# Turning the exponentials of a softmax through scratch memory and VectorE instead of through TensorE

## What is computed

```python
xn = group_norm(x, gamma, beta)
xf = xn.reshape(B, n, C)                       # n = H * W = 1024
q, k, v = xf @ Wq + bq, xf @ Wk + bk, xf @ Wv + bv
attn = jnp.einsum('bnc,bmc->bnm', q, k) * scale
attn = jax.nn.softmax(attn, axis=-1)
out = jnp.einsum('bnm,bmc->bnc', attn, v)
out = out @ Wp + bp
return xn + out.reshape(B, H, W, C)
```

## Time and profile before

| what | us |
|---|---|
| timed runs, median (lowest to highest) | 1071.11 (1070.84 to 1073.47) |
| profiled execution, its own time | 1070.88 |
| its span | 1068.9 |
| TensorE busy | 1023.6 (96%) |
| VectorE busy | 835.5 (78%) |
| ScalarE busy | 730.4 (68%) |
| GpSimd busy | 395.7 (37%) |

### The profile page before, as it was taken

One profiled execution on the slowest core, in us unless ns is written; L12 is line 12 of the kernel. 1 busy time (PEld: TensorE's weight loads), 2 busy tenths in 40 slices (PEclk: granted clock), 3 DMA queues, 4 the chain that ended last, 5 costly groups with the idle time before them and its releaser, 6 DMA issues.

```text
span 1068.9 us, 21353 instructions
## 1 busy us (share of the span) xinstructions
PE 1023.6 (96%) x7092; PEld 937.6 (88%) x7092; DVE 835.5 (78%) x1628; ACT 730.4 (68%) x1382; POOL 395.7 (37%) x366
## 2 busy tenths in 40 slices
PE   4989999999999999999999999999999999999997
PEld 3877889899898999989899898989989899898986
DVE  6868888778787877887878788877877787777774
ACT  1576866757675776857767685776767667677754
POOL 4535250533507144260623516053260714423021
PEclk9899999999999999999999999999999999999999
DMA  5101010010201001020100101001010100000001
GB/s 91 21 2 21 2 30 11 10 31 1 40 0 29 10 10 29 0 39 0 24 16 10 29 0 29 10 10 29 0 39 0 29 10 10 10 1 11 11 11 30
DMA packets 85637, 18.64 MB, mean 17 GB/s; under 512 B 67552, under 2 KB 85472, under 8 KB 85600
## 3 DMA queue, kind: packets, MB, share of 16 engines
q1 hardware_dynamic: 84752, 17.77, 8.8%
q10 hardware_dynamic: 848, 0.39, 0.2%
HBM read 9.76 MB, written 8.39 MB: 17 GB/s over the span
## 4 chain that ended last, share of the span: by engine, by line
issue 43%; PE 29%; POOL 13%; DVE 9%; ACT 4%; DMA 0%; POOLq 0%; SPq 0%; DVEq 0%; ACTq 0%
PE work L441 6%; PE work L443 5%; PE work L442 5%; PE ps_t L604 4%; POOL t_lo L1420 3%; POOL d L1426 2%; ACT et_hi L1042 2%; POOL xn_lo L1420 2%; PE work L500 2%; DVE d L1602 2%; POOL g_lo L1420 2%; POOL r_tok L1474 1%; POOL r_tok L1477 1%; PE ps_s L441 1%; PE ps_s L443 1%
## 5 line engine op out<-in xcount | busy, mean ns | idle before, releaser
L1420 POOL TENSOR_TENSOR g_lo<-u,g_hi 128x512 fp32r<-128x512 f32 x60 | 76.8, 1283 | 415.1 <-ACT g_hi L951 415.0
L1854 DVE TENSOR_TENSOR et_lo<-ps_t,et_hi 128x1024 fp32r<-128x1024 f32 x128 | 156.1, 1220 | 52.1 <-ACT et_hi L1042 51.6
L1042 ACT ACTIVATE et_hi<-ps_t 128x1024 fp32r<-128x1024 f32 x128 | 130.9, 1022 | 91.0 <-PE ps_t L604 87.8
L441 PE MATMUL work<-t_lo,wc_hi 128*128 128x256 f32 x576 | 173.4, 301 | 4.4 <-DVE wc_lo L1668 4.4
L1848 DVE TENSOR_REDUCE nm<-ps_s 128x1 f32<-128x1024 f32 x124 | 150.9, 1217 | 22.8 <-PE ps_s L443 20.5
L443 PE MATMUL work<-t_hi,wc_hi 128*128 128x256 f32 x576 | 162.8, 283 | 0.0
L442 PE MATMUL work<-t_hi,wc_lo 128*128 128x256 f32 x576 | 162.6, 282 | 0.0
L441 PE MATMUL work<-et_lo,vv_hi 128*128 128x256 f32 x512 | 147.9, 289 | 0.2 <-ACT a_all L1049 0.2
L1032 ACT ACTIVATE e<-ps_s,nm 128x1024 f32<-128x1024 f32 x124 | 138.1, 1114 | 11.7 <-DVE nm L1848 9.2
L443 PE MATMUL work<-et_hi,vv_hi 128*128 128x256 f32 x512 | 144.4, 282 | 0.0
L442 PE MATMUL work<-et_hi,vv_lo 128*128 128x256 f32 x512 | 144.1, 281 | 0.0
(11 more groups left out here) (184 smaller groups left out, 2415.7 us busy)
## 6 DMA issues: line engine op xcount, KB each, us to landing
x_in<-in_x SPq DMA_DIRECT2D x64, 128.0 KB, 3.4
out<-r_tok SPq DMA_DIRECT2D x32, 256.0 KB, 2.3
w_up_t<-in_L_conv_w_up SPq DMA_DIRECT2D x1, 384.0 KB, 3.8
const<-in_const ACTq DMA_DIRECT2D x1, 166.0 KB, 4.6
y<-in_L_conv_w_up ACTq DMA_DIRECT2D x1, 128.0 KB, 4.5
y<-in_L_conv_w_qkv SPq DMA_DIRECT2D x1, 128.0 KB, 4.7
const<-in_const ACTq DMA_DIRECT2D x1, 64.0 KB, 4.2
w_v<-in_L_conv_w_qkv SPq DMA_DIRECT2D x1, 64.0 KB, 2.8
```

Source lines behind the costliest of these rows:

```text
L441: te.matmul(dst, wh, xl, start=first, stop=False)
L1042: act.activation(et_hi[:, :, (t % 4) * 128:(t % 4 + 1) * 128], ps_t[:, :].rearrange("p (k c) -> p k c", k=TILES), ACT.Copy) \
L1420: return pool.tensor_tensor(dst, full, hi, ALU.subtract)
L1854: dve.tensor_tensor(et_lo[:, :, cols_], ps_t[:, :].rearrange("p (k c) -> p k c", k=TILES), et_hi[:, :, cols_].bitcast(F32), ALU.subtract). ...
```

## The change

The eight TensorE transposes of a tile go, and with them `probs_t` and its semaphore. There are two buffers `e`, two buffers `e_by_keys` and a scratch tensor of two blocks in device memory. `exp` writes its keys in another order (key b*128 + a*32 + i at column a*256 + b*32 + i). SyncE stores the tile to scratch memory (`move_out`, 512 KB, packets of 1 KB) and loads it back (`move_in`, rows of 4 KB) so that partition 32*a + j holds queries 4j to 4j+3 of key group a. VectorE turns that in 32 x 32 blocks into `et_f` (`et_turn`), which lies where `et_lo` lies. ScalarE makes the high half from `et_f`, and the low half is now subtracted in place by GpSimd. `ps_t` becomes the second score tile, so `scores(n, t)` waits for the exponential of tile t-2, and `exp(n, t)` for the turn of tile t-2. The wait for the `values` product that last read the tile moves from `et_hi_tile` to `et_turn`. The work banks are dealt out anew, and all five queues are ordered anew in fill, turn and drain. In ScalarE's turn the exponentials of tiles 6 and 7 now stand between the GELU steps 1 and 2. The load of the next image moves from between the two stores to the middle of the eight tiles. The diff, cut to the functions, SyncE's turn, and the new turns of the other engines where their order matters here:

```diff
-        e = sb("e", [128, PIX])
+        e = [sb(f"e_{k}", [128, PIX]) for k in range(2)]
+        e_by_keys = [sb(f"e_by_keys_{k}", [128, PIX]) for k in range(2)]
...
+        et_f = placed("et_f", [128, TILES, HALF], et_at + 4 * TILES * HALF)
...
-            return work_all[:, 0:PIX] if is_last(n) and t % 2 else ps_s
+            return (ps_s, ps_t)[t % 2]
...
+        e_blocks = nc.dram_tensor("e_blocks", (2, 128 * PIX), F32, kind="Internal").ap()
...
+            def move_out(n, t):
+                sp.wait_ge(*e_ready.after(n, t))
+                sp.dma_start(e_blocks[t % 2].rearrange("(a q m) -> q a m", a=4, q=128),
+                             e[t % 2][:, :].rearrange("q (a m) -> q a m", a=4)).then_inc(written[t % 2].handle, 16)
+
+            def move_in(n, t):
+                sp.wait_ge(*written[t % 2].after(n, t // 2))
+                sp.dma_start(e_by_keys[t % 2][:, :], e_blocks[t % 2].rearrange("(p c) -> p c", p=128)) \
+                  .then_inc(moved[t % 2].handle, 16)
...
             def turn_program(it):
-                a, d = it, it + 3
+                a, b, c, d = it, it + 1, it + 2, it + 3
+                move_out(a, 0)
+                move_in(a, 0)
+                move_out(a, 1)
+                move_in(a, 1)
+                move_out(a, 2)
+                move_out(a, 3)
+                move_in(a, 2)
+                move_in(a, 3)
+                load_x(d)
+                move_out(a, 4)
+                move_out(a, 5)
+                move_in(a, 4)
+                move_in(a, 5)
+                move_out(a, 6)
+                move_out(a, 7)
+                move_in(a, 6)
+                move_in(a, 7)
                 store(a, 0)
-                if has_next(d + 1):
-                    load_x(d + 1)
                 store(a, 1)
...
-                if not is_last(n) or t == 0:
-                    te.wait_ge(*e_ready.after(n, t - 1))
-                elif t % 2:
-                    te.wait_ge(*bank_free("s0", t, n))
-                    te.wait_ge(*bank_free("s1", t, n))
-                else:
-                    te.wait_ge(*e_ready.after(n, t - 2))
+                te.wait_ge(*e_ready.after(n, t - 2))
...
-            def probs_t(n, t):
-                te.wait_ge(*e_ready.after(n, t))
-                te.wait_ge(*et_lo_ready.after(n, t - 1))
-                for kt in range(TILES):
-                    mm = te.transpose(ps_t[:, kt * 128:(kt + 1) * 128], e[:, kt * 128:(kt + 1) * 128], ident)
-                mm.then_inc(pe["t"].handle, 1)
...
-                act.wait_ge(*pe["t"].after(n, t - 1))
+                act.wait_ge(*et_ready.after(n, t - 2))
...
-                act.activation(e[:, :], score_tile(n, t)[:, :], ACT.Exp, bias=nm1[:, t:t + 1], accum_out=sum1[:, t:t + 1]) \
-                   .then_inc(e_ready.handle, 1)
+                act.activation(e[t % 2][:, :].rearrange("p (a b i) -> p b a i", a=4, b=TILES),
+                               score_tile(n, t)[:, :].rearrange("p (b a i) -> p b a i", a=4, b=TILES), ACT.Exp,
+                               bias=nm1[:, t:t + 1], accum_out=sum1[:, t:t + 1]).then_inc(e_ready.handle, 1)
...
+                cols_ = slice((t % 4) * 128, (t % 4 + 1) * 128)
+                act.wait_ge(*et_ready.after(n, t))
+                act.activation(et_hi[:, :, cols_], et_f[:, :, cols_], ACT.Copy).then_inc(et_hi_ready.handle, 1)
...
+            def et_lo_tile(n, t):
+                cols_ = slice((t % 4) * 128, (t % 4 + 1) * 128)
+                pool.wait_ge(*et_hi_ready.after(n, t))
+                minus(et_lo[:, :, cols_], et_f[:, :, cols_], et_hi[:, :, cols_].bitcast(F32)).then_inc(et_lo_ready.handle, 1)
...
+            def et_turn(n, t):
+
+                dve.wait_ge(*moved[t % 2].after(n, t // 2))
...
+                if t % 2 == 0:
+                    dve.wait_ge(*pe["pv"].after(n, t // 2 - 2))
                 cols_ = slice((t % 4) * 128, (t % 4 + 1) * 128)
-                dve.wait_ge(*et_hi_ready.after(n, t))
-                dve.tensor_tensor(et_lo[:, :, cols_], ps_t[:, :].rearrange("p (k c) -> p k c", k=TILES),
-                                  et_hi[:, :, cols_].bitcast(F32), ALU.subtract).then_inc(et_lo_ready.handle, 1)
+                dve.transpose(et_f[:, :, cols_].rearrange("p b (j q) -> p q b j", q=4),
+                              e_by_keys[t % 2][:, :].rearrange("p (q b j) -> p q b j", q=4, b=TILES)) \
+                   .then_inc(et_ready.handle, 1)
```

More of the change, by code:

```diff
@@ L406, in fill_program @@
                 load_x(2)
+                move_out(0, 0)
+                move_in(0, 0)
+                move_out(0, 1)
+                move_in(0, 1)
+                move_out(0, 2)
+                move_in(0, 2)
+                move_out(0, 3)
+                move_in(0, 3)
+                move_out(0, 4)
+                move_in(0, 4)
+                move_out(0, 5)
+                move_out(0, 6)
+                move_in(0, 5)
+                move_in(0, 6)
                 load_x(3)
+                move_out(0, 7)
@@ L423, in drain_program @@
-                store(B - 2, 1)
+                move_out(B - 3, 0)
+                move_in(B - 3, 0)
+                move_out(B - 3, 1)
+                move_in(B - 3, 1)
+                move_out(B - 3, 2)
+                move_in(B - 3, 2)
+                move_out(B - 3, 3)
+                move_in(B - 3, 3)
+                move_out(B - 3, 4)
+                move_in(B - 3, 4)
+                move_out(B - 3, 5)
+                move_in(B - 3, 5)
+                move_out(B - 3, 6)
+                move_in(B - 3, 6)
@@ new lines, in drain_program @@
+                move_out(B - 3, 7)
+                store(B - 3, 0)
+                move_in(B - 3, 7)
+                move_out(B - 2, 0)
+                move_in(B - 2, 0)
+                move_out(B - 2, 1)
+                move_in(B - 2, 1)
+                move_out(B - 2, 2)
+                move_in(B - 2, 2)
+                move_out(B - 2, 3)
+                move_in(B - 2, 3)
+                move_out(B - 2, 4)
+                store(B - 3, 1)
+                move_in(B - 2, 4)
+                move_out(B - 2, 5)
@@ new lines, in drain_program @@
+                move_in(B - 2, 5)
+                move_out(B - 2, 6)
+                move_in(B - 2, 6)
+                move_out(B - 2, 7)
+                move_in(B - 2, 7)
+                move_out(B - 1, 0)
+                store(B - 2, 0)
+                move_out(B - 1, 1)
+                move_in(B - 1, 0)
+                move_in(B - 1, 1)
+                move_out(B - 1, 2)
+                move_out(B - 1, 3)
+                move_in(B - 1, 2)
+                move_in(B - 1, 3)
+                store(B - 2, 1)
@@ L424, in drain_program @@
+                move_out(B - 1, 4)
+                move_out(B - 1, 5)
+                move_in(B - 1, 4)
+                move_in(B - 1, 5)
+                move_out(B - 1, 6)
+                move_out(B - 1, 7)
+                move_in(B - 1, 6)
+                move_in(B - 1, 7)
                 store(B - 1, 0)
                 store(B - 1, 1)
-            fill_program()
-            turn_program(1)
-            with sp.Fori(2, B - 4) as it:
-                turn_program(it)
-            turn_program(B - 4)
@@ L655, in fill_program @@
                 v(0, 0)
+                up2(0, 1)
                 q(0, 0)
-                up2(0, 1)
                 k(0, 0)
@@ L712, in fill_program @@
                 up2(2, 0)
[L713 to L715 removed]
+                scores(0, 7)
+                group_moments(1)
+                values(0, 1)
                 v(2, 0)
[L717 to L724 removed]
@@ new lines, in drain_program @@
+                scores(B - 2, 0)
+                scores(B - 2, 1)
+                q(B - 1, 1)
+                k(B - 1, 1)
+                v(B - 1, 1)
+                scores(B - 2, 2)
+                qq(B - 2, 1)
+                local_scores(B - 1, 0)
+                local_scores(B - 1, 1)
+                values(B - 3, 2)
+                local_scores(B - 1, 2)
+                scores(B - 2, 3)
+                local_probs_t(B - 1, 0)
+                values(B - 3, 3)
+                local_probs_t(B - 1, 1)
@@ new lines, in fill_program @@
+                local_exp(1, 1)
+                local_scale(1, 0)
+                take(2, 0, 1)
+                exp(0, 1)
+                t_hi_part(2, 1)
+                q_half(1, 1)
+                local_scale(1, 1)
+                pt_pair(1, 0)
+                exp(0, 2)
+                pt_pair(1, 1)
+                local_exp(1, 2)
+                et_hi_tile(0, 0)
+                t_hi_part(2, 2)
+                local_scale(1, 2)
+                take(2, 2, 3)
+                local_exp(1, 3)
```

1065 lines of the change are left out of this document (513 added, 552 removed), and 59 rows, old and new, of tables (BANK_PLAN, DRAIN_PLAN, FILL_PLAN).

## The result

The changed kernel takes 1147.66 us (1146.09 to 1149.64), against 1071.14 us for the kernel before in the same comparison: 1.071 times as long, interval 1.0685 to 1.0735. It is slower, as forecast (1124 us), by 77 us where 53 were forecast; the time lies in both ranges. The profiled execution took 1146.43 us, its span is 1144.6.

What follows compares the result with a forecast made beforehand. TensorE bounds the kernel before (62.7 of 63.66 us a turn). After, VectorE's turn is 60.2 + 3 + 3.5 = 66.7: twelve turns +36, fill +4, last image +13, so +53 on 1070.88: 1124 us, range 1005 to 1175.

Steps and rivals of the forecast that it cites:

- VectorE becomes the bound: Main loop: VectorE's work grows from 51.2 to 60.2 us a turn plus 3 of holds, above TensorE's 54.4.
- the row on which the forecast rested: The new transpose's row on VectorE, said to decide: 2.3 us or 1.25.
- The transpose: VectorE's eight new transposes a turn: 2.35 us each with the 16-byte store step, between 1.25 and 2.35.
- The holds: Combine steps and channel_moments on VectorE, held by running GpSimd operations: 3 us a turn, 0 to 12.
- The round trip: Scratch memory: store 3.0 us, load 3.9, circle 10.95; VectorE idle some 3.5 us a turn (0 to 8).
- TensorE's floor: TensorE's work in a turn after losing 64 transposes: 62.7 - 8.3 = 54.4 us.
- The last image: From its first row maximum's end to the end: 55 us after 42, so +13 us (0 to +20).
- Fill and the two images before the last: Outside the loop's turns: fill +4 us (-5 to +10), the two images before the last nothing.
- Full rate with holds: Rival: full-rate transposes, but holds and in-order waits eat the gain; turn about 62 us, 1055 (1030 to 1075); chance 0.18.
- Full rate with TensorE as the bound: Rival: the 16-byte step costs nothing, TensorE stays the bound; turn 57 us, 990 (976 to 1005); chance 0.15.
- Slow scratch memory: Rival: a store and the load behind it take 5 us each; turn 73 us, 1210 in all; chance 0.10.

Runs made afterwards that it cites:

- e1: The changed kernel with the transposes storing over neighbours and a_part putting the queries back in order; 1094.54 us, 1.0213 of before.
- e2: The changed kernel with GpSimd's subtraction of a tile cut into four pieces of 256 columns; 1113.68 us, 1.0396 of before.
- e3: The changed kernel with both the transposes stored over neighbours and GpSimd's subtraction in four pieces; 1077.18 us, 1.0048 of before.
- e9: As e3, but exponentials wait for the store of two tiles before, three load buffers (eight in the last image), three high halves moved earlier; 1061.92 us, 0.9901 of before.
- e4: The changed kernel without the store to scratch memory, the load back and their waits (attention not the reference's); one execution, 1110.91 us.
- e6: As e1, but all eight low halves of a turn subtracted on VectorE instead of GpSimd; 1187.21 us, 1.1083 of before.

## Why the forecast was right, and where it was off

*VectorE becomes the bound.* Right: it works 62.5 of 67.8 us, where 60.2 + 3 = 63.2 were forecast, and the edits that only shorten its instructions (e1, e2, e3) shorten the turn. The step of the transpose alone doesn't decide the sign, though. e1 undoes the row on which the forecast rested, and 53 of 77 us go, but the kernel stays slower than before; only with shorter holds it comes level (e3), and only with buffers set free earlier it gets ahead (e9).

*The transpose.* I put 2.35 us between bounds of 1.25 and 2.35; it is 2.04. The step costs (2037 - 1236) / 1024 = 0.78 ns a column, not the 1.07 of the step of 32 bytes. The cacheline rule of the Trainium skill ("SBUF — State Buffer", the cachelines in its specifications) names the right side, and gives no size for the penalty; here the transpose takes 1.65 times as long. The transpose mode's "one element per cycle per lane" ("Vector Engine (DVE) Microarchitecture Reference") fits here only the store over neighbours: 1.24 us, 1.03 ns for each column beyond the 512 of the earlier trace rows.

*The holds.* I took 3 us from 0 to 12 for five operations; busy time over counts is 62.5 - 57.7 = 4.8. My own average, half of 2.35 us each, gives 5.9 for five, and 3.5 to 4.7 with one or two that find GpSimd idle, so 3 was low by my own rule. By their means the four combine steps and channel_moments are 3.9 us a turn longer than before. I had not listed the two one-column steps of group_norm (L1889, L1891): 0.16 and 0.22 us before, 1.14 and 1.02 after, held by h_lo and g_lo, which the new orders put beside them, 1.8 us a turn. And channel_moments was held nearly every time (median 1.98 us). The transposes were 2.5 us a turn too dear in the forecast and the holds 1.8 too cheap; that VectorE's busy time came out within 0.7 us (62.5 for 63.2) is luck in part.

*The round trip.* 3.2 and 3.8 us for 3.0 and 3.9 (the rows of 64 and 384 KB, drawn on in a straight line, give 4.2 to 4.3; my 3.9 was close by chance). VectorE's idle time is 5.3 us a turn, not 3.5, within its bounds; e4 gives the loads 2.0 of it, less than the forecast's 3.5. The rest are short waits for ScalarE, GpSimd and TensorE in the same queue, which the forecast didn't list. That is the term that makes the turn 67.8 and not 66.7, and with twelve turns 14 of the 23 us that the forecast was low.

*TensorE's floor* of 54.4 us was too low. The 8.3 us are a union, and in it the last transposes of a tile overlap the product behind them. In the kernel before, in order of time:

```profile
479.75 1.03 PE L604 MATMUL ps_t<-const,e 128*128 128x128 f32 x8
480.63 0.86 PE L514 MATMUL work<-kp,q_all 128*128 128x204 f32 x4
```

From the first transpose to that product it is 0.88 us, not 1.03; over the eight tiles of a turn it is 6.9 us, and the floor 55.8. The time didn't hang on it, since VectorE stood above both.

*GpSimd* at 2.46 us a low half (2.35) and 44.4 a turn (43), *ScalarE* at 46.9 (47.4): right.

*The last image.* 61.7 us, forecast 55. The circles are 11.4 and 12.3 us (10.95), as the row maxima of tiles 2 (at 1086.0), 4 and 6 show, and behind the last transpose 14.2 us pass, where my steps gave 10.7. There TensorE waits for GpSimd's last low half and then runs at its lower clock; the last 24 products take from 1133.9 to 1139.0, 5.1 us and not 2.8:

```profile
1131.00:1133.00 2.00, 0.00 (x0) 0.00 (x0) 0.62 (x4) 0.44 (x1) 1.79 (x2) 0.63 0.26 70
...
1135.00:1137.00 2.00, 2.00 (x11) 2.00 (x11) 0.00 (x0) 0.00 (x0) 1.56 (x2) 0.50 0.00 0
```

Hence +19.5 and not +13.

*Fill and the two images before the last.* +4 to +6, forecast +4.

*TensorE's clock* was not in the forecast. In the turn shown it falls to its lower level while TensorE waits for held steps of VectorE. TensorE is not the bound there, and what this costs a turn was not tried by itself; e2 and e3 show turns at 1.00. In the last image, where `output` waits for TensorE, it costs about the 2.3 us above.

*The rivals.* Full rate with holds (1055, 1030 to 1075) has e1's kernel as its case, and VectorE is busy 56.1 us there, as it said (51.4 + 5). But the turn is 64.6 us, not 62, and the time 1094.5, above its range; only with shorter holds (e3, 1077) does a run come near it. Full rate with TensorE as the bound (990) came out in no run, not even without the trip (1043). Slow scratch memory falls by the 3.2 and 3.8 us.

## What to carry to other kernels

Before moving work from a full engine to one with room, price it on the new engine with its store pattern: a permutation that is free in the address can make the instruction take two thirds longer (2.04 us for 1.24), and it may be pushed to a reader for which it is free (here ScalarE's copy from PSUM). Next, list every instruction of VectorE with two SBUF inputs, the one-column ones too, that a long GpSimd instruction can run beside, since each can lose up to that whole instruction. Then look for the waits: when no engine was busy much over 90% here, setting buffers free earlier won 1.3 us a turn (e9). And a step put late in an in-order queue can cost more than its own time: in e6 a low half of 1.2 us stands so late that `output` waits 4.4.
